# Quantised window attention and a ConvNeXt block on one core: the order of VectorE's five instructions within an attention step

## The chip, the cores and the metric

The kernel runs on one NeuronCore of a Trainium2 chip. A core has five engines, each with a queue of its own that it works through strictly in order: TensorE (PE in the profile, PEld for its weight loads), VectorE (DVE), ScalarE (ACT), GpSimd (POOL) and SyncE (SP, which here only issues transfers). They meet through semaphores alone. The metric is the device time of one execution, in microseconds (us), as the median of several runs; lower is better.

## The reference

The input is 16 images of 192 channels and 56 x 56 pixels. Two layers follow each other: window attention with simulated 8-bit quantisation, then a ConvNeXt block (7x7 depthwise convolution, layer norm, two linear layers, GELU and a response norm). Only the attention is touched, and of it only this core:

```python
attn = jnp.einsum('bhmc,bhnc->bhmn', q, k)     # 12 heads, windows of 7x7 = 49 tokens
bias = fq(bias, axis=0)
attn = fq(attn) + bias[None]                   # fq: round to 8 bits with the maximum of all elements
attn = fq(attn)
attn = jax.nn.softmax(attn, axis=3)
out = jnp.einsum('bhmn,bhnc->bhmc', attn, v)
```

There are 16 x 64 windows. Softmax needs, for each row of 49, the maximum, the exponentials, their sum and a division.

## The kernel before

The program is a row of phases: input, the ranges of q, k and v, their quantisation, the range of the products, **attention**, projection, convolution, MLP. Each phase is a block; its engines' programs are written out by hand, and nothing reorders them.

Attention handles two windows at once (49 of each 64 partitions) for all twelve heads: a tile is 128 partitions by 588 columns. One such pair of windows is an item, 16 items are a unit, and there are 32 units, so 512 items. A loop turn on every engine is two units, 32 steps long and written out in full. In step n each engine does its stages for different items, given by `LAG_A2, LAG_MX, LAG_L, LAG_E, LAG_PV, LAG_N = 1, 2, 3, 4, 6, 7`. In step n:

- TensorE, in this order: the products q k of item n into `p_psum` (line 551 in a helper); the shifted logits of item n-3 into `l_psum` (lines 842 to 846: the logits and the negated maxima are added up by matmuls with the identity), which wait for the maxima of n-3; the 24 matmuls with v for item n-6 into `o_psum` (line 861), which wait for the division of n-7, since there is a single `o_psum`, and for GpSimd's part of n-6; and the transposes of item n-1 into `t_psum` (line 870), which wait for the logits of n-1 and for the maxima of n-2, since there is a single `t_psum`.
- ScalarE: two exponentials of item n-4, to f32 (889) and to f16 (890), and then the rounding of item n to int8, `attn_int` (896).
- GpSimd: `exp_lo`, the difference of the two exponentials of item n-4, in two instructions (819).
- VectorE: the **logits** of item n-1, `logit_int` (915), which read two tiles in SBUF (`attn_int` and the bias) and wait for ScalarE's rounding; the **reciprocals** of the twelve sums of item n-7 (924), which wait for its matmuls with v (semaphore `pv_done`); the **maxima** of item n-2 (930), which read `t_psum` and wait for its transposes (`transposed`); the **division** of item n-7 (939), which reads `o_psum` and writes `a_o` (`norm_done`). After every fourth division a reduction over four items, `o_stat` (945), is taken, and after every sixteenth two tiny instructions more (948 and 950), which let the unit's result be stored.

SyncE loads q, k and v a unit ahead and stores the results; what it waits for are ends of units.

Of the kernel before, what the change touches and what calls it, by code (L numbers as in the profile page):

```python
# [7 lines left out]
ALU = mybir.AluOpType  # L8
# [5 lines left out]
P = 128  # L14
# [6 lines left out]
HEADS, HD = 12, 16  # L21
# [6 lines left out]
UP = UB * PAIRS  # L28
# [32 lines left out]
def chain(eng, sem, start=0):  # L61

    count = [start]

    def link(ins):
        count[0] += 1
        ins.then_inc(sem, 1)
        eng.wait_ge(sem, count[0])
    link.count = count
    return link  # L70
# [46 lines left out]
def col(s, k, rows=P):  # L117
    return s.sc[0:rows, k:k + 1]
# [601 lines left out]
PV0 = 2 * (HD + 1)  # L720

LAG_A2, LAG_MX, LAG_L, LAG_E, LAG_PV, LAG_N = 1, 2, 3, 4, 6, 7
# [7 lines left out]
def phase_attention(s):  # L730

    nc = s.nc
    H1 = HD + 1
    CHUNKS = [(0, 0), (128, 0), (256, 0), (384, 0), (HM - P, 512 - (HM - P))]
    with ExitStack() as c:
# [4 lines left out]
        o = [sb(f"a_o{k}", [P, UP, 2, CK], F32) for k in range(2)]  # L740
# [6 lines left out]
        rec = sb("sum_recip", [P, 12], F32)  # L747
# [5 lines left out]
        po = pb("o_psum", [P, 512], F32)  # L753
        ld = [s.sem(f"a_qk_loaded{k}") for k in range(2)]
        lv = [s.sem(f"a_v_loaded{k}") for k in range(2)]
        st = [s.sem(f"a_stored{k}") for k in range(2)]
# [3 lines left out]
        hid, lod, pvd, nrm = s.sem("hi_done"), s.sem("lo_done"), s.sem("pv_done"), s.sem("norm_done")  # L760
        recd, ostd, ch, ar = s.sem("recip_done"), s.sem("o_stat_done"), s.sem("p4_chain"), s.sem("o_allmax")
# [3 lines left out]
        def steps(eng, step):  # L765

            def turn(i, first):
                for k in range(2):
                    for j in range(UP):
                        step(32 * i + 16 * k + j, 16 * k + j, lambda lag: not first or 16 * k + j >= lag)  # L770
            peeled(eng, IMG, turn)
            for j in range(LAG_N):
                step(TAIL + j, j, lambda lag: lag > j)

        @blk.sync
        def _(sp):
            def store(u, k):
                sp.wait_ge(ostd, u + 1)
                for h in range(2):
                    sp.dma_start(s.od[bass.ds(u, 1)].rearrange("u h n j w f -> (u h) n j w f")[h], o[k][64 * h:64 * h + N]).then_inc(st[k], 16)  # L780

            def unit(i, first):
                for k in range(2):
                    u = bass.ds(2 * i + k, 1)
                    if not first:
                        sp.wait_ge(qk, UP * (2 * i + k - 1))
                    load_qk(s, sp, u, q[k], kt[k], ld[k])
                    if not first:
                        sp.wait_ge(pvd, UP * (2 * i + k - 1))
                    else:  # L790
                        sp.wait_ge(vzero, k + 1)
                    for w in range(2):
                        sp.dma_start(vt[k][64 * w:64 * w + N, w], s.vd[bass.ds(2 * i + k, 1)].rearrange("u o n j f -> (u o) n j f")[w]).then_inc(lv[k], 16)
                    if not first:
                        store(2 * i + k - 2, k)
            peeled(sp, IMG, unit)
            for k in range(2):
                store(UNITS - 2 + k, k)
            for k in range(2):
                sp.wait_ge(st[k], 32 * IMG)  # L800
# [100 lines left out]
        @blk.vector  # L901
        def _(dve):
            v = nc.vector
            v.memset(orun[:], 0.0).then_inc(recd, 1)
            for m in vt + o:
                v.memset(m[:], 0.0).then_inc(vzero, 1)
            dve.wait_ge(vzero, 4)

            def step(n, l, stage):
                if stage(LAG_A2):  # L910
                    m, r = n - LAG_A2, (l - LAG_A2) % 4
                    dve.wait_ge(a1d, m + 1)
                    if stage(LAG_A2 + 4):
                        dve.wait_ge(lgd, m - 3)
                    v.scalar_tensor_tensor(a2[r][:], a1[(l - LAG_A2) % 2][:], col(s, RAT), s.bpart[:], ALU.mult, ALU.add).then_inc(a2d, 1)  # L915
                if stage(LAG_N):
                    m, lm = n - LAG_N, (l - LAG_N) % (2 * UP)
                    k, j = lm // UP, lm % UP
                    dve.wait_ge(pvd, m + 1)
                    if stage(LAG_N + 1):  # L920
                        dve.wait_ge(nrm, m)
                    if j == 0 and stage(LAG_N + 2 * UP):
                        dve.wait_ge(st[k], m - lm)
                    v.reciprocal(rec[:], po[:, 0:12 * H1].rearrange("p (x c) -> p x c", c=H1)[:, :, HD]).then_inc(recd, 1)
                if stage(LAG_MX):
                    m, r = n - LAG_MX, (l - LAG_MX) % 4
                    dve.wait_ge(td, m + 1)
                    if stage(LAG_MX + 4):
                        dve.wait_ge(lgd, m - 3)
                    v.tensor_reduce(nmx[r][:], pt[:, 0:5].rearrange("p c (w n) -> p c w n", w=2)[:, :, :, 0:N], AX.X, ALU.max,  # L930
                                    negate=True).then_inc(mxd, 1)
                if stage(LAG_N):
                    m, lm = n - LAG_N, (l - LAG_N) % (2 * UP)
                    k, j = lm // UP, lm % UP
                    dve.wait_ge(recd, m + 2)
                    src = po[:, 0:6 * PV0].rearrange("p (b w c) -> p b w c", b=6, w=2)[:, :, :, 0:HD]
                    rr = rec[:].rearrange("p (b w) -> p b w", b=6).unsqueeze(3).broadcast_to([P, 6, 2, HD])
                    dst = o[k][:, j].rearrange("p w (b c) -> p b w c", b=6)
                    v.tensor_tensor(dst, src, rr, ALU.mult).then_inc(nrm, 1)  # L939
                if stage(LAG_N):  # L940
                    m, lm = n - LAG_N, (l - LAG_N) % (2 * UP)
                    k, j = lm // UP, lm % UP
                    if j % 4 == 3:
                        dve.wait_ge(nrm, m + 1)
                        v.tensor_reduce(ost[:, j // 4:j // 4 + 1], o[k][:, j - 3:j + 1], AX.XYZ, ALU.max, apply_absolute_value=True).then_inc(ch2, 1)
                    if j == UP - 1:
                        dve.wait_ge(ch2, 5 * unit_of(n, l) + 4)
                        v.tensor_tensor(orun[:], orun[:], ost[:], ALU.max).then_inc(ch2, 1)
                        dve.wait_ge(ch2, 5 * unit_of(n, l) + 5)
                        v.memset(mark[:], 0.0).then_inc(ostd, 1)  # L950

            def unit_of(n, l):

                m, lm = n - LAG_N, (l - LAG_N) % (2 * UP)
                return (m - lm) // UP + lm // UP

            ch2 = s.sem("o_stat_chain")
            mark = sb("mark", [1, 1], F32)
            steps(dve, step)
            dve.wait_ge(ostd, UNITS)  # L960
            link = chain(dve, ch)
            link(v.memset(col(s, T0), 0.0))
            for p0 in (0, 64):
                link(v.tensor_reduce(s.sc[p0:p0 + N, T0:T0 + 1], orun[p0:p0 + N, :], AX.X, ALU.max))
            dve.wait_ge(ar, 1)

            link(v.tensor_tensor(col(s, T1), col(s, T1), col(s, SV), ALU.mult))
            link(v.tensor_scalar(col(s, T1), col(s, T1), AMIN, None, ALU.max))
            link(v.tensor_scalar(col(s, SO), col(s, T1), 1.0 / QMAX, None, ALU.mult))
            link(v.reciprocal(col(s, T2), col(s, T1)))  # L970
            link(v.tensor_tensor(col(s, T2), col(s, T2), col(s, SV), ALU.mult))
            link(v.tensor_scalar(col(s, INVO), col(s, T2), QMAX, None, ALU.mult))
# [876 lines left out]
```

## Time and profile before

| | us |
|---|---|
| median of 3 runs | 5552.63 (5549.53 to 5571.55) |
| profiled execution | 5547.89, span of its trace 5545.9 |
| first and last start of the logits (L915) | 1595.4, 2912.2 |
| VectorE busy in the whole span | 4244.0 (77%) |
| TensorE busy in the whole span | 4071.9 (73%) |
| ScalarE busy | 2965.2 (53%) |
| GpSimd busy | 1516.8 (27%) |

The span is the time from the first to the last instruction of the trace. Attention takes about a quarter of it. The page's chain of what ended last covers other phases, so attention must be read from the order in time of its own instructions: a start, a duration, and in brackets how long the engine was idle before it and who ended that. On VectorE an instruction may start before the recorded end of the one ahead, by some 0.08 us, so steps are measured from start to start.

### The profile page before, as it was taken

To read this page: it belongs to the slowest core of one execution; us is meant where nothing else is said; L and a number is where in the kernel's file an instruction comes from. 1 tells how busy PE (TensorE), PEld (TensorE's weight loads), DVE (VectorE), ACT (ScalarE), POOL (GpSimd) and SP (SyncE) were. 2 spreads that over 40 slices of the span, in tenths; PEclk is the share of its full clock that TensorE was granted. 3 is DMA by queue.
4 is the path that set the end of the run, shared out by engine and by line. 5 is a ranking of instruction groups with operands and counts; after the bars stand their busy time and mean duration, and the time that the engine had idled before them with its cause. 6 is when DMAs were issued, how large, how long until landed. Compare 5 with 4: busy or idle time off the path is not lost. (4 is left out here: it accounts for less than half of the span.)

```text
span 5545.9 us, 116266 instructions
## 1 busy us (share of the span) xinstructions
PE 4071.9 (73%) x40394; PEld 2582.2 (47%) x40394; DVE 4244.0 (77%) x6728; ACT 2965.2 (53%) x5218; POOL 1516.8 (27%) x1842
## 2 busy tenths in 40 slices
PE   0786783444447787777784665999668999999999
PEld 0333453333336666666663443444334454545454
DVE  6898997999989888888895554000189999999985
ACT  0764660000048787787782655444356666666664
POOL 0103330000036555565563221000122222222220
PEclk9998885555579999999996777999879999999999
DMA  7864763333323333333224777788512222222222
GB/s 299 220 180 138 224 220 85 65 66 70 70 54 83 80 79 83 78 80 83 77 67 158 249 273 254 268 289 292 184 63 81 82 84 79 84 80 86 80 75 63
DMA packets 227818, 724.20 MB, mean 131 GB/s; under 512 B 30347, under 2 KB 128139, under 8 KB 206795
## 3 DMA queue, kind: packets, MB, share of 16 engines
q1 hardware_dynamic: 203402, 589.58, 36.5%
q0 software_dynamic: 24128, 130.26, 6.5%
q8 instruction: 245, 4.01, 0.3%
q14 instruction: 43, 0.34, 0.0%
HBM read 428.25 MB, written 291.50 MB: 130 GB/s over the span
## 5 line engine op out<-in xcount | busy, mean ns | idle before, releaser
L819 POOL TENSOR_TENSOR exp_lo<-exp,exp_hi 128x294 f16<-128x294 f32 x1024 | 774.7, 780 | 553.7 <-ACT exp_hi L890 549.8
L896 ACT ACTIVATE attn_int<-p_psum,scalars 128x588 int8<-128x588 f32 x512 | 384.6, 751 | 995.7 <-PE p_psum L551 969.3
L1581 PE MATMUL out_psum<-gelu_hi,w_parts 128*128 128x448 f16 x2016 | 605.7, 355 | 58.1 <-DVE w_parts L1757 30.7
L915 DVE SCALAR_TENSOR_TENSOR logit_int<-attn_int,scalars,bias_products 128x588 f16<-128x588 int8 x512 | 506.3, 989 | 117.7 <-ACT attn_int L896 88.5
L633 PE MATMUL range_psum<-q_diag,k_diag 128*128 128x196 bf16 x1536 | 293.2, 369 | 369.1 <-DVE p_min L679 362.6
L1653 DVE BATCH_NORM_STATS2 ln_stats<-z_img 128x6 f32<-128x192 f32 x448 | 126.0, 344 | 564.2 <-DMA z_img<-zd 563.6
L1617 ACT ACTIVATE gelu_pair<-h_psum,b_rows,w_unscale 128x448 f32<-128x448 f32 x448 | 325.0, 729 | 414.5 <-PE h_psum L1533 249.8
L861 PE MATMUL o_psum<-a_v,exp_hi 128*128 128x34 f16 x6144 | 383.1, 179 | 193.5 <-DVE a_o L939 183.0
L1317 PE MATMUL conv_psum<-c_in,toeplitz 128*128 128x448 f16 (+1 forms) x2304 | 469.3, 366 | 67.4 <-DMA dwb<-in_L_conv_dw_b_dram 67.3
L1533 PE MATMUL h_psum<-ln_parts_T,w_hi 128*128 128x448 f16 x2016 | 494.7, 354 | 18.5 <-DVE w_in L1716 16.5
L1581 PE MATMUL out_psum<-gelu_lo,w_parts 128*128 128x448 f16 x1344 | 476.0, 354 | 0.0
L861 PEld LDWEIGHTS o_psum<-a_v,exp_hi 128*128 128x128 f16 x6144 | 340.5, 96 | 245.8 <-issue 200.2
L633 PEld LDWEIGHTS range_psum<-q_diag,k_diag 128*128 128x128 bf16 x1536 | 223.7, 161 | 438.3 <-DVE p_min L679 428.8
L889 ACT ACTIVATE exp<-l_psum,scalars 128x588 f32<-128x588 f32 x512 | 382.0, 746 | 32.1 <-PE l_psum L846 28.7
L1474 POOL TENSOR_TENSOR ln_parts<-ln_out,ln_parts 128x512 f16<-128x512 f32 x224 | 257.2, 1168 | 504.3 <-DVE ln_parts L1681 504.3
L890 ACT ACTIVATE exp_hi<-l_psum,scalars 128x588 f16<-128x588 f32 x512 | 393.0, 767 | 0.0
L1331 ACT ACTIVATE c_out<-conv_psum,dwb,conv_unscale 128x448 f32<-128x448 f32 x192 | 223.6, 1165 | 312.7 <-PE conv_psum L1317 312.7
L861 PE MATMUL o_psum<-a_v,exp_lo 128*128 128x34 f16 x6144 | 381.2, 179 | 1.5 <-issue 1.5
L1317 PEld LDWEIGHTS conv_psum<-c_in,toeplitz 128*128 128x128 f16 x2304 | 223.6, 98 | 312.9 <-DMA dwb<-in_L_conv_dw_b_dram 41.1
L1533 PE MATMUL h_psum<-ln_parts_T,w_lo 128*128 128x448 f16 x1344 | 365.8, 354 | 0.0
L930 DVE TENSOR_REDUCE neg_max<-t_psum 128x10 f16<-128x490 f16 x512 | 327.1, 639 | 28.7 <-PE t_psum L870 16.3
L861 PEld LDWEIGHTS o_psum<-a_v,exp_lo 128*128 128x128 f16 x6144 | 337.8, 96 | 7.8 <-issue 7.0
(313 smaller groups left out, 9684.7 us busy)
## 6 DMA issues: line engine op xcount, KB each, us to landing
k_diag<-kd SPq DMA_DIRECT2D x128, 384.0 KB, 5.3
toeplitz<-gd SPq DMA_DIRECT2D x48, 1024.0 KB, 16.8
yd<-y_out POOLq DMA_DIRECT2D x16, 2880.0 KB, 28.0
c_in<-yd SPq DMA_DIRECT2D x24, 1920.0 KB, 9.5
zd<-c_out POOLq DMA_DIRECT2D x24, 1792.0 KB, 13.9
z_img<-zd SPq DMA_DIRECT2D x16, 2688.0 KB, 9.4
x_chunk<-in_x_dram SPq DMA_DIRECT2D x12, 3136.0 KB, 9.9
x_img<-in_x_dram SPq DMA_DIRECT2D x16, 2352.0 KB, 16.0
```

The source lines that it names most:

```text
L633: last = nc.tensor.matmul(ps[:, x % 2, y // 2, y % 2 * 256:y % 2 * 256 + HG * N], kt[k][:, g].rearrange("p o n -> p (o n)")[:, j::UP], q[k ...
L819: last = nc.gpsimd.tensor_tensor(el[r][:, :, 2 * a, 0:N], src[:, :, a], eh[r][:, :, 2 * a, 0:N], ALU.subtract)
L861: last = nc.tensor.matmul(po[:, b * PV0:(b + 1) * PV0], x[r][:, b, a:a + 2].rearrange("p a n -> p (a n)"), rhs, start=a == 0 and x is eh, ...
L889: nc.scalar.activation(e[r % 2][:], pl[:, bank, 0:HM], ACT.Exp, scale=col(s, S2))
L890: nc.scalar.activation(eh[r][:, :, 0:3:2].rearrange("p b a n -> p a b n")[:, :, :, 0:N], pl[:, bank, 0:HM].rearrange("p (a b n) -> p a b n ...
L896: nc.scalar.activation(a1[l % 2][:].rearrange("p (g n) -> p g n", g=G), pp[:, 0:G, 0:HG * N], ACT.Copy, scale=col(s, CP)).then_inc(a1d, 1)
L915: v.scalar_tensor_tensor(a2[r][:], a1[(l - LAG_A2) % 2][:], col(s, RAT), s.bpart[:], ALU.mult, ALU.add).then_inc(a2d, 1)
L930: v.tensor_reduce(nmx[r][:], pt[:, 0:5].rearrange("p c (w n) -> p c w n", w=2)[:, :, :, 0:N], AX.X, ALU.max, negate=True).then_inc(mxd, 1)
L1317: last = nc.tensor.matmul(out[:, :, lo:hi], tp[k][:, w, ch, 2 - d, :], yi[k][:, :, ch, yy, lo + d:hi + d], start=x == 0 and part == 0, sto ...
L1533: last = nc.tensor.matmul(ph[:, y % 3, 0:TCH], w, xx, start=x == 0, stop=x == 4)
L1581: last = nc.tensor.matmul(po[:, t, 0:TCH], w, hx[:, f, cols], start=f == 0 and x == 0, stop=f == NF - 1 and x == len(steps) - 1)
L1617: nc.scalar.activation(h[y // 2 % 3][:, y % 2], ph[:, y % 3, 0:TCH], ACT.Gelu, scale=k1[:], bias=b1[:, f:f + 1]).then_inc(hd, 1)
```

## The change

VectorE's instructions within a step are written in another order. Before: logits, reciprocals, maxima, division. After: reciprocals, logits, division, maxima. Every instruction keeps its operands and its waits; no buffer, no lag and no other engine's program changes. `o_stat` stays last in its step.

```diff
             def step(n, l, stage):
+                if stage(LAG_N):
+                    m, lm = n - LAG_N, (l - LAG_N) % (2 * UP)
+                    k, j = lm // UP, lm % UP
+                    dve.wait_ge(pvd, m + 1)
+                    if stage(LAG_N + 1):
+                        dve.wait_ge(nrm, m)
+                    if j == 0 and stage(LAG_N + 2 * UP):
+                        dve.wait_ge(st[k], m - lm)
+                    v.reciprocal(rec[:], po[:, 0:12 * H1].rearrange("p (x c) -> p x c", c=H1)[:, :, HD]).then_inc(recd, 1)
                 if stage(LAG_A2):
...
-                    dve.wait_ge(pvd, m + 1)
-                    if stage(LAG_N + 1):
-                        dve.wait_ge(nrm, m)
-                    if j == 0 and stage(LAG_N + 2 * UP):
-                        dve.wait_ge(st[k], m - lm)
-                    v.reciprocal(rec[:], po[:, 0:12 * H1].rearrange("p (x c) -> p x c", c=H1)[:, :, HD]).then_inc(recd, 1)
+                    dve.wait_ge(recd, m + 2)
+                    src = po[:, 0:6 * PV0].rearrange("p (b w c) -> p b w c", b=6, w=2)[:, :, :, 0:HD]
...
+                    v.tensor_tensor(dst, src, rr, ALU.mult).then_inc(nrm, 1)
                 if stage(LAG_MX):
...
-                if stage(LAG_N):
...
-                    v.tensor_tensor(dst, src, rr, ALU.mult).then_inc(nrm, 1)
```

VectorE's queue before, in a step that ends with the reduction over four items and at the start of the next. Here L915 is the logits, L924 the reciprocals, L930 the maxima, L939 the division, L945 the reduction:

```order
L915 SCALAR_TENSOR_TENSOR logit_int<-attn_int,scalars,bias_products 128x588 [waits logits_done,a1_done]
L924 RECIPROCAL sum_recip<-o_psum 128x12 [waits norm_done,pv_done]
L930 TENSOR_REDUCE neg_max<-t_psum 128x10 [waits logits_done,transposed]
L939 TENSOR_TENSOR a_o<-o_psum,sum_recip 128x6x2x16 [waits recip_done]
L945 TENSOR_REDUCE o_stat<-a_o 128x1 [waits norm_done]
L915 SCALAR_TENSOR_TENSOR logit_int<-attn_int,scalars,bias_products 128x588 [waits logits_done,a1_done]
```

The same place after the change, where the lines are L918 for the reciprocals, L924 for the logits, L932 for the division and L938 for the maxima:

```order
L918 RECIPROCAL sum_recip<-o_psum 128x12 [waits norm_done,pv_done]
L924 SCALAR_TENSOR_TENSOR logit_int<-attn_int,scalars,bias_products 128x588 [waits logits_done,a1_done]
L932 TENSOR_TENSOR a_o<-o_psum,sum_recip 128x6x2x16 [waits recip_done]
L938 TENSOR_REDUCE neg_max<-t_psum 128x10 [waits logits_done,transposed]
L945 TENSOR_REDUCE o_stat<-a_o 128x1 [waits norm_done]
L918 RECIPROCAL sum_recip<-o_psum 128x12 [waits norm_done,pv_done]
```

The logits now stand between the reciprocals and the division, the maxima behind the division, and a step begins with the wait for the matmuls with v (`pv_done`) instead of the wait for the rounding (`a1_done`).

## Rows read from the trace of the kernel before

**Rows 1.** First line of the page.

```profile
span 5545.9 us, 116266 instructions
```

**Rows 2.** Busy time of the engines over the attention stretch, with its columns.

```profile
core 0: us, PE busy (x) PEld busy (x) DVE busy (x) ACT busy (x) POOL busy (x), PEclk, DMA share, GB/s
1595.00:2926.00 1331.00, 1043.45 (x22524) 844.48 (x22522) 1153.37 (x2243) 1053.65 (x1535) 774.66 (x1024) 0.95 0.31 78
```

**Rows 3.** Waits in the attention stretch: us in total, times, longest us.

```profile
PE o_psum L861 <- DVE a_o L939: 183.0, 437, 1.8
```

**Rows 4.** The reductions over four items, all of them: durations, first and last start.

```profile
L945 DVE TENSOR_REDUCE o_stat<-a_o x128: 952/953/955, 1615.0 to 2924.5; 128x1 f32<-128x768 f32 x128
```

**Rows 5.** Instructions of VectorE in time, one group of four steps: start us, us.

```profile
2112.34 0.34 DVE L939 TENSOR_TENSOR a_o<-o_psum,sum_recip 128x192 f32<-128x192 f32 x1
2112.70 0.95 DVE L945 TENSOR_REDUCE o_stat<-a_o 128x1 f32<-128x768 f32 x1
2113.57 0.82 DVE L915 SCALAR_TENSOR_TENSOR logit_int<-attn_int,scalars,bias_products 128x588 f16<-128x588 int8 x1
2114.31 0.23 DVE L924 RECIPROCAL sum_recip<-o_psum 128x12 f32<-128x12 f32 x1
2114.45 0.61 DVE L930 TENSOR_REDUCE neg_max<-t_psum 128x10 f16<-128x490 f16 x1
2114.98 0.34 DVE L939 TENSOR_TENSOR a_o<-o_psum,sum_recip 128x192 f32<-128x192 f32 x1
2115.24 1.05 DVE L915 SCALAR_TENSOR_TENSOR logit_int<-attn_int,scalars,bias_products 128x588 f16<-128x588 int8 x1
...
2116.55 0.67 DVE L930 TENSOR_REDUCE neg_max<-t_psum 128x10 f16<-128x490 f16 x1
2117.14 0.35 DVE L939 TENSOR_TENSOR a_o<-o_psum,sum_recip 128x192 f32<-128x192 f32 x1
...
2118.42 0.23 DVE L924 RECIPROCAL sum_recip<-o_psum 128x12 f32<-128x12 f32 x1
...
2121.57 0.33 DVE L939 TENSOR_TENSOR a_o<-o_psum,sum_recip 128x192 f32<-128x192 f32 x1
```

**Rows 6.** The same steps: TensorE's matmuls with v and transposes; then GpSimd's rows.

```profile
2117.63 0.18 PE L861 MATMUL o_psum<-a_v,exp_hi 128*128 128x34 f16 x1 [0.22 <-DVE a_o L939]
...
2118.23 0.44 PE L870 MATMUL t_psum<-ident_f,logit_int 128*128 128x128 f16 x5
...
2114.04 1.62 POOL L819 TENSOR_TENSOR exp_lo<-exp,exp_hi 128x294 f16<-128x294 f32 x2 [0.75 <-ACT exp_hi L890]
...
2121.11 1.41 POOL L819 TENSOR_TENSOR exp_lo<-exp,exp_hi 128x294 f16<-128x294 f32 x2 [0.75 <-ACT exp_hi L890]
```

**Rows 7.** Three meetings of the logits with GpSimd, from VectorE's and GpSimd's instructions in time.

```profile
2103.81 1.94 POOL L819 TENSOR_TENSOR exp_lo<-exp,exp_hi 128x294 f16<-128x294 f32 x2 [0.75 <-ACT exp_hi L890]
2103.82 1.35 DVE L915 SCALAR_TENSOR_TENSOR logit_int<-attn_int,scalars,bias_products 128x588 f16<-128x588 int8 x1
...
2106.02 0.81 DVE L915 SCALAR_TENSOR_TENSOR logit_int<-attn_int,scalars,bias_products 128x588 f16<-128x588 int8 x1
2106.05 2.06 POOL L819 TENSOR_TENSOR exp_lo<-exp,exp_hi 128x294 f16<-128x294 f32 x2 [0.30 <-ACT exp_hi L890]
...
1601.83 1.94 POOL L819 TENSOR_TENSOR exp_lo<-exp,exp_hi 128x294 f16<-128x294 f32 x2 [9.04 <-ACT exp_hi L890]
1602.33 0.86 DVE L915 SCALAR_TENSOR_TENSOR logit_int<-attn_int,scalars,bias_products 128x588 f16<-128x588 int8 x1 [0.76 <-ACT attn_int L896]
```

**Rows 8.** VectorE at the end of a unit.

```profile
2102.47 0.95 DVE L945 TENSOR_REDUCE o_stat<-a_o 128x1 f32<-128x768 f32 x1
```

**Rows 9.** VectorE after the stop at a loop turn.

```profile
2088.29 0.83 DVE L915 SCALAR_TENSOR_TENSOR logit_int<-attn_int,scalars,bias_products 128x588 f16<-128x588 int8 x1 [5.29 <-ACT attn_int L896]
2089.26 0.23 DVE L924 RECIPROCAL sum_recip<-o_psum 128x12 f32<-128x12 f32 x1
...
2090.38 0.35 DVE L939 TENSOR_TENSOR a_o<-o_psum,sum_recip 128x192 f32<-128x192 f32 x1
```

More of the change, by code:

```diff
@@ L918, in step @@
                     k, j = lm // UP, lm % UP
-                    dve.wait_ge(pvd, m + 1)
-                    if stage(LAG_N + 1):
-                        dve.wait_ge(nrm, m)
-                    if j == 0 and stage(LAG_N + 2 * UP):
-                        dve.wait_ge(st[k], m - lm)
-                    v.reciprocal(rec[:], po[:, 0:12 * H1].rearrange("p (x c) -> p x c", c=H1)[:, :, HD]).then_inc(recd, 1)
+                    dve.wait_ge(recd, m + 2)
+                    src = po[:, 0:6 * PV0].rearrange("p (b w c) -> p b w c", b=6, w=2)[:, :, :, 0:HD]
+                    rr = rec[:].rearrange("p (b w) -> p b w", b=6).unsqueeze(3).broadcast_to([P, 6, 2, HD])
+                    dst = o[k][:, j].rearrange("p w (b c) -> p b w c", b=6)
+                    v.tensor_tensor(dst, src, rr, ALU.mult).then_inc(nrm, 1)
                 if stage(LAG_MX):
@@ L931, in step @@
                                     negate=True).then_inc(mxd, 1)
-                if stage(LAG_N):
[L933 to L938, printed above, removed]
-                    v.tensor_tensor(dst, src, rr, ALU.mult).then_inc(nrm, 1)
                 if stage(LAG_N):
```

## The prediction

> **What bounds the kernel now.** The first view is the busy time by stretch: in the 1331 us of attention VectorE is busy for 1153, ScalarE for 1054, TensorE for 1043 [rows 2]. No engine is full, so a loop of waits between them sets the pace. The second view is the waits: TensorE stands 183.0 us, in 437 of 512 steps, before its matmuls with v until VectorE's division is done [rows 3]. The change brings that division forward, past the maxima. What it pays is read from the third view, the instructions in time.
>
> All numbers of a step are distances from start to start. I call the start of a division N. From N, the matmuls with v start 0.49 later (2117.14 to 2117.63) [rows 5, 6]; the transposes start 1.09 after N (2118.23), are 0.44 long, and the next maxima start 0.04 after that, at N + 1.57 (2114.98 to 2116.55) [rows 5, 6]; the next division is 0.59 after them (2116.55 to 2117.14) [rows 5]. So **before** there is a loop division, matmuls with v, transposes, maxima, division, of 1.57 + 0.59 = 2.16 us, and 2114.98 to 2117.14 is just that. Of the other loop, the reciprocals may start at N + 1.28 (2117.14 to 2118.42), the end of the matmuls with v [rows 5].
>
> A group of four steps, from the division ahead of one reduction to that ahead of the next, is 2112.34 to 2121.57 = 9.23 [rows 5]: the step with the reduction takes 2.64 (2112.34 to 2114.98), two take 2.16, one takes 2.27, in which the logits stood behind GpSimd. 68 of the 96 groups that do not hold a unit's end take 9.22 to 9.30; the mean over all is (2924.5 - 1615.0) / 127 = 10.31 [rows 4], since 15 loop turns hold a stop of some 5 us [rows 9] and 31 groups a unit's end.
>
> **The change part by part.** Nothing is added or removed; 512 steps are reordered.
>
> *The loop that goes.* The maxima no longer stand ahead of the division. They run at N + 0.26 (as 2114.98 to 2115.24 for what followed a division without waiting) and are over at about N + 0.87, before the transposes that need their buffer (N + 1.09) and before the shifted logits, which come after those. They are hidden under the 1.28 us of the matmuls with v. The loop of 2.16 is gone.
>
> *The loop that takes its place.* The logits now stand between the reciprocals and the division: reciprocals, 0.15 (0.14 in 2114.31 to 2114.45, and 0.01 for a start out of a wait), logits, 0.74 (2113.57 to 2114.31), division, 1.28 or 1.29, reciprocals. Sum 0.15 + 0.74 + 1.29 = **2.18 us** [rows 5], against 2.16. A plain step thus gains nothing: the 0.59 of the maxima left the loop and the 0.74 of the logits entered it, while the 0.29 between the ends of the two TensorE stages was won.
>
> *The step with the reduction.* After N: 0.26, maxima 0.52 (2114.45 to 2114.98 pipelined), reduction 0.87 (2112.70 to 2113.57), reciprocals 0.14, logits at N + 1.79, division at N + 2.53 if nothing stops them [rows 5]. That is 0.11 less than the 2.64 of before. Four steps: 2.53 + 3 x 2.18 = 9.07, which is 0.16 under 9.23.
>
> *What stops the logits.* The logits and GpSimd's two instructions don't run at the same time. Logits that start 0.01 after GpSimd take 1.35 instead of 0.82, and GpSimd 1.94 instead of 1.41; logits that start 0.03 before GpSimd take 0.81 and GpSimd 2.06; logits that start 0.50 after it, near the end of its first instruction, slip between the two: 0.86 [rows 7]. So a tie costs 0.53, while to be 0.03 ahead or 0.50 behind costs nearly nothing. The Trainium skill, SBUF — State Buffer, in its section on the ports, says the same in kind: a VectorE instruction with two inputs in SBUF and a GpSimd instruction exclude each other for a whole instruction, and who starts first has the port. By a bandwidth that is merely shared the sum would be the 9.07 above in every group; by the page's lock it hangs on who is first, and the trace agrees with the lock (1.35 against 0.82). What follows uses the rows only.
>
> GpSimd starts 3.97 after the division two of its steps back (2117.14 to 2121.11) [rows 5, 6], since that division releases, through TensorE, the rounding and then the exponentials; the change leaves this chain as it is. In plain steps the logits start at N + 1.43 + 2.18 = N + 3.61, thus 0.36 before GpSimd: free. After a reduction, GpSimd comes 3.97 - 2.18 = 1.79 after N, and the logits at N + 1.79: **a tie**, to within what I can read. By the first row pair of [rows 7] I give it to GpSimd: + 0.54. Then division at N + 3.07; the following logits at 3.07 + 1.44 = 4.51, which is 0.54 after GpSimd's 3.97, so between its two instructions; the third and fourth steps are free. Group: 3.07 + 3 x 2.18 = **9.61**, + 0.38 on 9.23.
>
> *The ends of units.* From the reduction to the next logits it is 2102.47 to 2103.82 = 1.35, and to the next reduction (2112.70) 10.23, with a tie in it [rows 5, 7, 8]; 9 groups read so, 13 are 0.5 shorter, without the tie, and 9 longer. After: 0.26 + 0.52 + 1.35 + 0.14 = N + 2.27 for the logits, 0.48 behind GpSimd: it slips in for 0.04. Division at 3.05, group 3.05 + 6.54 = 9.59. Gain 0.64 in 9, 0.13 in 13, and I take 0.3 in the other 9: 5.8 + 1.7 + 2.7 = 10 us.
>
> *The loop turns.* TensorE stops for about 5 us; before, the first reciprocals (2089.26) wait for the matmuls with v, the maxima for the transposes, and the division starts at 2090.38, 1.12 later [rows 9]. After it is 0.15 + 0.74 = 0.89: 0.23 less, and the next step starts without the wait for transposes. I take 0.4 for each of 15: 6 us. The logits wait longer there for the reciprocals, but are ready in time.
>
> **Sum.** 68 groups x 0.38 = + 26; ends of units - 10; loop turns - 6; 13 disturbed groups at half the tie + 2: **+ 12 us**. The trace's span of 5545.9 [rows 1] lies 2.0 under its own execution's time of 5547.89, which gives 5560; the median of the runs is 4.7 above that execution: about **5564 us**.
>
> **The rivals.**
> *Who wins the tie: VectorE.* Then the group is 9.07 and 68 x 0.16 = 11 us are gained, with 10 and 6 as above and 1 for the others: - 28, 5525 us. For it: the two starts are equal by my rows, and 0.03 ahead is enough. Against: 0.01 or 0.02 more anywhere in the loop pulls GpSimd forward relative to the logits. Since by this case the next step is a tie again, it needs all ties.
> *Starts that cost more.* The maxima take 0.67 out of a wait and 0.61 without (0.59 and 0.53 to the division) [rows 5]: 0.06 for a start out of a wait. If the reciprocals, which now wait in each step, hand this to the logits, 512 x 0.06 = + 31: 5595 us.
> *The gap is missed: slower.* After a lost tie the next logits arrive 0.54 after GpSimd's start; I have seen 0.50 slip in. If the second GpSimd instruction (0.7 long) is already in, they wait till shortly before its end (in the tie 0.53 were waited for a first instruction of 1.41 / 2 = 0.7, so 0.2 before it): 1.41 - 0.2 - 0.54 = 0.67, and the step behind meets GpSimd's first instruction for 0.2 more. The group is then some 10.5, + 1.25 x 68 = 85, less 14: + 71, 5624 us. It decides at the point where the logits arrive later than about 0.6 after GpSimd.
> *The wait for the division was worth its 183 us.* If TensorE's wait were the bound, moving the division by 0.59 would give 0.3 or more in each step, 150 us. Against it: TensorE waits for a division that itself waits for the matmuls one step earlier; I give it 2 in 100.
>
> **How the numbers follow.** Forecast with the tie lost 0.50; tie won 0.22; dearer starts 0.14; gap missed 0.12; the large gain 0.02. A measurement of this kernel can tell about 0.5%, or 28 us, from no change: 5525 and 5580 are the bounds. The forecast lies within them; the tie won lies on the lower bound, half of it is counted as faster (0.11), and with the large gain and surprises of that sign I say 0.17. Slower: dearer starts, gap missed and a little of the forecast's upper end, 0.30. The rest, 0.53, is within. The range takes in the tie won with some margin and the dearer starts, 5515 to 5602, and leaves out the missed gap and the large gain.
>
> **What the profile after would show.** Plain steps of 2.17 to 2.20 between divisions; maxima starting 0.26 after the division; reciprocals always waiting for the matmuls with v; TensorE's wait for the division smaller in no great measure, since the loop is as long; the logits behind the reduction of about 1.35 (tie lost) or 0.82 (tie won); those one step later 0.82 to 0.86 (gap) or 1.4 (missed). The forecast is wrong if plain steps are not near 2.18, or if GpSimd no longer starts 3.97 after a division.

## The result and the profile after

The changed kernel takes 5644.02 us (median of 4 runs, 5626.26 to 5646.43), the kernel before 5558.41 in the same comparison: ratio 1.0145, 95% interval 1.0114 to 1.0176. It is slower, by about 86 us between the medians, and lies above the predicted range, which ended at 5602. The profiled execution has a span of 5641.8, 95.9 more than that of before [rows 1].

First, where the time lies. The busy times of the attention stretch and the 128 reductions over four items (columns as in [rows 2] and [rows 4]) of the changed kernel:

```profile
1595.00:3030.00 1435.00, 1052.87 (x22522) 852.53 (x22522) 1142.57 (x2251) 1053.10 (x1535) 908.70 (x1027) 0.93 0.29 73
```

```profile
L945 DVE TENSOR_REDUCE o_stat<-a_o x128: 934/942/953, 1614.0 to 3015.8; 128x1 f32<-128x768 f32 x128
```

From the first to the last reduction it is now 1401.8 us, before 1309.5: 92 of the 96 us are in this loop. VectorE, ScalarE and TensorE are as busy as before to within 1% (1143, 1053, 1053 us); only GpSimd has gone from 775 to 909. Its rows on the two pages, first before, then after (busy us, mean ns | idle before):

```profile
L819 POOL TENSOR_TENSOR exp_lo<-exp,exp_hi 128x294 f16<-128x294 f32 x1024 | 774.7, 780 | 553.7 <-ACT exp_hi L890 549.8
```

```profile
L819 POOL TENSOR_TENSOR exp_lo<-exp,exp_hi 128x294 f16<-128x294 f32 x1024 | 905.6, 907 | 514.4 <-ACT exp_hi L890 510.7
L924 DVE SCALAR_TENSOR_TENSOR logit_int<-attn_int,scalars,bias_products 128x588 f16<-128x588 int8 x512 | 501.2, 979 | 2.2 <-ACT attn_int L896 2.2
```

The logits have not become longer: 979 ns on average, 989 before. Without GpSimd's subtractions they take 816 and 827 ns (experiments 2 and 1), so what they wait for GpSimd inside their own duration is the same in both orders, some 0.16 us each or 83 us over 512. It has moved to a place where it counts.

The waits in the attention stretch (us in total, times, longest) show the new loop: the reciprocals now stand before the matmuls with v, and TensorE still stands before the division, longer than before [rows 3]:

```profile
DVE sum_recip L918 <- PE o_psum L861: 272.4, 402, 6.6
PE o_psum L861 <- DVE a_o L932: 250.5, 426, 1.8
```

**Two patterns.** Of the 96 groups of four steps without a unit's end, 24 take 9.6 to 9.85 us and 27 take 10.4 to 10.6 (before, 66 took 9.2 to 9.35). Here is one of the first kind, VectorE in time (start us, us), with the first two instructions of GpSimd that it meets behind it. Compare [rows 5]:

```profile
1783.24 0.35 DVE L932 TENSOR_TENSOR a_o<-o_psum,sum_recip 128x192 f32<-128x192 f32 x1
1783.51 0.66 DVE L938 TENSOR_REDUCE neg_max<-t_psum 128x10 f16<-128x490 f16 x1
1784.08 0.94 DVE L945 TENSOR_REDUCE o_stat<-a_o 128x1 f32<-128x768 f32 x1
1784.94 0.22 DVE L918 RECIPROCAL sum_recip<-o_psum 128x12 f32<-128x12 f32 x1
1785.08 1.29 DVE L924 SCALAR_TENSOR_TENSOR logit_int<-attn_int,scalars,bias_products 128x588 f16<-128x588 int8 x1
1786.29 0.34 DVE L932 TENSOR_TENSOR a_o<-o_psum,sum_recip 128x192 f32<-128x192 f32 x1
...
1787.58 0.23 DVE L918 RECIPROCAL sum_recip<-o_psum 128x12 f32<-128x12 f32 x1 [0.37 <-PE o_psum L861]
1787.75 0.83 DVE L924 SCALAR_TENSOR_TENSOR logit_int<-attn_int,scalars,bias_products 128x588 f16<-128x588 int8 x1
1788.50 0.35 DVE L932 TENSOR_TENSOR a_o<-o_psum,sum_recip 128x192 f32<-128x192 f32 x1
...
1792.91 0.35 DVE L932 TENSOR_TENSOR a_o<-o_psum,sum_recip 128x192 f32<-128x192 f32 x1
```

```profile
1785.01 1.94 POOL L819 TENSOR_TENSOR exp_lo<-exp,exp_hi 128x294 f16<-128x294 f32 x2 [0.42 <-ACT exp_hi L890]
1787.21 1.96 POOL L819 TENSOR_TENSOR exp_lo<-exp,exp_hi 128x294 f16<-128x294 f32 x2 [0.26 <-ACT exp_hi L890]
```

The logits behind the reduction (1785.08) lose the tie against GpSimd (1785.01) and take 1.29; the next (1787.75) start 0.54 after GpSimd and slip between its two instructions, 0.83. The distances between divisions are 3.05, 2.21, 2.20, 2.21, in all 9.67. This is the predicted pattern (9.61), to 0.06.

And here is one of the second kind, which the prediction does not have:

```profile
2229.64 0.34 DVE L932 TENSOR_TENSOR a_o<-o_psum,sum_recip 128x192 f32<-128x192 f32 x1
...
2231.09 1.35 DVE L924 SCALAR_TENSOR_TENSOR logit_int<-attn_int,scalars,bias_products 128x588 f16<-128x588 int8 x1
2232.37 0.34 DVE L932 TENSOR_TENSOR a_o<-o_psum,sum_recip 128x192 f32<-128x192 f32 x1
...
2233.83 1.14 DVE L924 SCALAR_TENSOR_TENSOR logit_int<-attn_int,scalars,bias_products 128x588 f16<-128x588 int8 x1
2234.89 0.34 DVE L932 TENSOR_TENSOR a_o<-o_psum,sum_recip 128x192 f32<-128x192 f32 x1
...
2236.34 1.36 DVE L924 SCALAR_TENSOR_TENSOR logit_int<-attn_int,scalars,bias_products 128x588 f16<-128x588 int8 x1
2237.63 0.34 DVE L932 TENSOR_TENSOR a_o<-o_psum,sum_recip 128x192 f32<-128x192 f32 x1
```

```profile
2231.09 1.94 POOL L819 TENSOR_TENSOR exp_lo<-exp,exp_hi 128x294 f16<-128x294 f32 x2 [0.79 <-ACT exp_hi L890]
2233.61 1.94 POOL L819 TENSOR_TENSOR exp_lo<-exp,exp_hi 128x294 f16<-128x294 f32 x2 [0.58 <-ACT exp_hi L890]
2236.34 1.94 POOL L819 TENSOR_TENSOR exp_lo<-exp,exp_hi 128x294 f16<-128x294 f32 x2 [0.80 <-ACT exp_hi L890]
```

Steps alternate: 2.73, 2.52, 2.74, and 2.51 to the next. (That next step holds a reduction, and keeps the rhythm: behind a step of 2.74 GpSimd starts early, and the logits come 0.62 after it, at 2239.47 against 2238.85, and slip in between its two instructions.) GpSimd still starts 3.97 after a division (2229.64 to 2233.61, 2232.37 to 2236.34). So a step of length P puts the logits after it at N + P + 1.46 against GpSimd at N + 3.97. If P is 2.52 that is a tie, 0.53 is waited, and the step becomes 2.21 + 0.53 = 2.74. After a step of 2.74 the logits come 0.22 after GpSimd and wait the remaining 0.3: 2.52, and the next is a tie again. Two steps in a row sum to 2.21 + (3.97 - 1.46) + 0.53 = 5.25. In 134 places of the trace two steps in a row, each over 2.4, sum to 5.23 to 5.29; in 3 places before. (Both must be over 2.4, since 3.05 + 2.21 of the first kind gives 5.26 too.) **The waiting keeps itself alive**: each wait lengthens the step by just what makes the next logits meet GpSimd again. Plain steps of 2.21 don't meet it (0.3 ahead), but nothing inside the pattern leads back to them except the chance that a tie falls the other way.

**Where the second kind starts: at the loop turns.** TensorE's stop there makes a step of 7 to 8.5 us. The second step behind it holds a reduction. Here is one turn, VectorE and then GpSimd:

```profile
2201.69 0.23 DVE L918 RECIPROCAL sum_recip<-o_psum 128x12 f32<-128x12 f32 x1 [5.79 <-PE o_psum L861]
...
2207.26 0.76 DVE L924 SCALAR_TENSOR_TENSOR logit_int<-attn_int,scalars,bias_products 128x588 f16<-128x588 int8 x1
...
2209.40 1.37 DVE L924 SCALAR_TENSOR_TENSOR logit_int<-attn_int,scalars,bias_products 128x588 f16<-128x588 int8 x1
```

```profile
2207.28 4.06 POOL L819 TENSOR_TENSOR exp_lo<-exp,exp_hi 128x294 f16<-128x294 f32 x4 [0.50 <-ACT exp_hi L890]
```

The logits behind the reduction start together with GpSimd and win (0.76, and the step is 2.52); the next ones lose (1.37). So it goes almost every time: the step with the reduction is 2.52 behind all 14 such stops, in 12 of them with a start within 0.03 of GpSimd's, and in 13 the alternation follows. Five of the 13 end in the same group, when a tie falls to VectorE. The other eight last until an irregular stop of TensorE, the next turn or the end.

**The end of a unit** is the third finding. Before, behind the reduction of [rows 8]:

```profile
2103.46 0.16 DVE L948 TENSOR_TENSOR o_run<-o_run,o_stat 128x4 f32<-128x4 f32 x1
```

After (VectorE, then GpSimd):

```profile
2169.51 0.94 DVE L945 TENSOR_REDUCE o_stat<-a_o 128x1 f32<-128x768 f32 x1
2170.49 0.70 DVE L948 TENSOR_TENSOR o_run<-o_run,o_stat 128x4 f32<-128x4 f32 x1
2171.25 0.06 DVE L950 MEMSET mark<- 1x1 f32 x1
```

```profile
2170.44 1.41 POOL L819 TENSOR_TENSOR exp_lo<-exp,exp_hi 128x294 f16<-128x294 f32 x2 [0.42 <-ACT exp_hi L890]
```

The running maximum over units (948), four columns wide, also reads two tiles in SBUF. With the maxima ahead of it, it starts with GpSimd and takes 0.69 to 0.71 instead of 0.16, in 20 of the 32 units. The median step at a unit's end is 3.72 us, against 3.05 predicted.

A second loss hangs on it. Here are such a step and the two behind it (columns as in [rows 2]; the third number from the end is the granted clock):

```profile
1772.14:1775.86 3.72, 2.17 (x54) 1.68 (x48) 3.60 (x8) 3.57 (x6) 2.76 (x4) 1.00 0.44 142
1775.86:1778.08 2.22, 1.73 (x33) 1.74 (x34) 1.83 (x5) 0.18 (x1) 1.41 (x2) 0.73 0.46 179
1778.08:1781.03 2.95, 2.95 (x49) 2.10 (x49) 1.84 (x5) 2.37 (x4) 0.23 (x1) 0.63 0.45 183
```

TensorE is busy for only 2.17 of the 3.72 us, then the granted clock falls for a while from 1.00 to 0.50 (from the level of 2.4 GHz to that of 1.2), TensorE is busy throughout, and a step takes 2.95 instead of 2.21. This happens behind 12 of the 31 ends, all with the long step, and costs some 8 us; before, it happens behind 5.

### The profile page after: what moved, and what is told of

Read it like the earlier page. It is cut to its first block and busy times, and to the rows that moved or that the text cites. A ratio compares the mean times of both kernels' runs of the same rounds, so it can differ in the third digit from the quotient of the medians.

```text
span 5641.8 us, 116266 instructions
## 1 busy us (share of the span) xinstructions
PE 4085.3 (72%) x40394; PEld 2593.7 (46%) x40394; DVE 4230.7 (75%) x6728; ACT 2965.3 (53%) x5218; POOL 1649.2 (29%) x1842
## 5 line engine op out<-in xcount | busy, mean ns | idle before, releaser
L819 POOL TENSOR_TENSOR exp_lo<-exp,exp_hi 128x294 f16<-128x294 f32 x1024 | 905.6, 907 | 514.4 <-ACT exp_hi L890 510.7
L924 DVE SCALAR_TENSOR_TENSOR logit_int<-attn_int,scalars,bias_products 128x588 f16<-128x588 int8 x512 | 501.2, 979 | 2.2 <-ACT attn_int L896 2.2
L679 DVE TENSOR_TENSOR p_max<-range_psum,p_max 128x1568 f32<-128x1568 f32 x192 | 341.2, 1777 | 0.0
```

What stands on the lines that cost most here:

```text
L679: v.tensor_tensor(e[:, g], ps[:, x % 2].rearrange("p a (b c) -> p (a b) c", b=2)[:, :, 0:HG * N], e[:, g], op).then_inc(done, 1)
L819: last = nc.gpsimd.tensor_tensor(el[r][:, :, 2 * a, 0:N], src[:, :, a], eh[r][:, :, 2 * a, 0:N], ALU.subtract)
```

## The experiments

Each kernel was timed beside the kernel before; ratios are to that, with their 95% intervals. Theory A: logits and GpSimd's subtractions exclude each other and fall into step. Rival B: the new loop is slow by itself.

**1 and 2: no subtractions.** In both orders, GpSimd's two instructions become one on a single element; the kernels leave out the low part of the exponentials.

```diff
-                    for a in range(2):
-                        last = nc.gpsimd.tensor_tensor(el[r][:, :, 2 * a, 0:N], src[:, :, a], eh[r][:, :, 2 * a, 0:N], ALU.subtract)
+                    last = nc.gpsimd.tensor_tensor(tick[:, r:r + 1], tock[:], tock[:], ALU.subtract)
```

> The kernel before, with GpSimd's two subtractions per step replaced by one on a single element; the low part of the exponentials stays zero, so that part of the computation is left out. Theory A (the changed kernel is slow because logits and GpSimd's subtractions exclude each other and fall into step): before loses its few waits too, a group of four steps is 2.64 + 3 x 2.16 = 9.12 instead of 9.24, time some 10 to 25 us under the kernel before. Rival B (the new loop through the logits is slow by itself, GpSimd plays no part): within 5 us of before.

> The changed order, with the same part left out: GpSimd's subtractions are one on a single element. Theory A: the difference between the orders vanishes: plain steps 2.21, the step with the reduction 2.51, group 9.14, time within 15 us of the run before without subtractions. Rival B: the changed order stays 60 us or more slower than it.

Before without subtractions: 5526.07 us, 0.997 (0.9948 to 0.9992). Changed without subtractions: 5536.35 us, 0.9988 (0.997 to 1.0006). The 1.45% have become 0.2%, with intervals that overlap; from first to last reduction it is 1297.0 us in the changed order,

```profile
L945 DVE TENSOR_REDUCE o_stat<-a_o x128: 939/943/953, 1615.6 to 2912.6; 128x1 f32<-128x768 f32 x128
```

and 1295.7 in the order of before. The group of four reads as theory A has it, 2.52 + 2.21 + 2.20 + 2.21 = 9.14:

```profile
1777.11 0.35 DVE L932 TENSOR_TENSOR a_o<-o_psum,sum_recip 128x192 f32<-128x192 f32 x1
...
1779.63 0.35 DVE L932 TENSOR_TENSOR a_o<-o_psum,sum_recip 128x192 f32<-128x192 f32 x1
...
1781.84 0.35 DVE L932 TENSOR_TENSOR a_o<-o_psum,sum_recip 128x192 f32<-128x192 f32 x1
...
1784.04 0.35 DVE L932 TENSOR_TENSOR a_o<-o_psum,sum_recip 128x192 f32<-128x192 f32 x1
...
1786.25 0.35 DVE L932 TENSOR_TENSOR a_o<-o_psum,sum_recip 128x192 f32<-128x192 f32 x1
```

Rival B has fallen. These two don't tell which instruction of VectorE is stopped, only that GpSimd's work is needed for the loss. It could also reach the loop another way, since TensorE's weight loads for the matmuls with v wait for `exp_lo`. That wait was 38.6 us in all before and is 55.1 in the changed kernel, so this way explains at most 17 of the 92 us. Nearly all of it lies at units' ends, and it is gone in experiment 9.

**3 and 4: the same subtractions in one, and in four instructions**, in the changed order.

```diff
+                    last = nc.gpsimd.tensor_tensor(el[r][:, :, 0:3:2, 0:N], src, eh[r][:, :, 0:3:2, 0:N], ALU.subtract)
...
+                    for a in range(2):
+                        for b in (0, 3):
+                            last = nc.gpsimd.tensor_tensor(el[r][:, b:b + 3, 2 * a, 0:N], src[:, b:b + 3, a], eh[r][:, b:b + 3, 2 * a, 0:N], ALU.subtract)
```

> The changed order, GpSimd's two subtractions in one instruction of twice the size. Theory A: two steps in a row sum to 2.21 + (3.97 - 1.45) + h, h being what a tie costs; h grows from 0.53 to about 1.2, so steps alternate around 2.95 instead of 2.63 wherever they are in step, and the tie behind a reduction costs 1.2: 60 to 120 us slower than the changed kernel, 5700 to 5760. Rival B: no change, 5640.

> The changed order, GpSimd's subtractions in four instructions of half the size. Theory A: h is about 0.2; a step of 2.52 is followed by one of 2.4, which is too short to meet GpSimd again, so steps fall back to 2.21 and a group is 9.2 to 9.5: 5550 to 5590. Rival B: no change, 5640, or slower by GpSimd's added instructions.

One instruction: 5696.21 us, 1.0256 (1.0203 to 1.0308), just under the expected 5700. The tie now costs 1.0 (logits of 1.82 that start 0.07 after GpSimd, so 1.06 for a full tie; VectorE, then GpSimd):

```profile
1751.03 1.82 DVE L923 SCALAR_TENSOR_TENSOR logit_int<-attn_int,scalars,bias_products 128x588 f16<-128x588 int8 x1
```

```profile
1750.96 1.27 POOL L818 TENSOR_TENSOR exp_lo<-exp,exp_hi 128x588 f16<-128x588 f32 x1 [0.55 <-ACT exp_hi L889]
```

24 groups read 11.6, steps of 3.06 and 2.73 in turn: a pair of 5.79, where 4.72 + 1.06 = 5.78. Four instructions: 5568.9 us, 1.0045 (1.0026 to 1.0064), within the expectation. The most common group is 2.77 + 3 x 2.21 = 9.4, and no two steps over 2.4 sum to 5.23 to 5.29. The same work in other pieces moves the time over 127 us, in the way the wait for one piece of it says.

**5 and 9: the end of a unit.** First the element's write behind the running maximum was suspected, then the running maximum itself.

```diff
-                        v.memset(mark[:], 0.0).then_inc(ostd, 1)
+                        v.tensor_reduce(mark[:], ost[0:1, :], AX.X, ALU.max).then_inc(ostd, 1)
...
-                        v.tensor_tensor(orun[:], orun[:], ost[:], ALU.max).then_inc(ch2, 1)
+                        v.tensor_reduce(both[1 - k][:, 1], both[k][:].rearrange("p a b -> p b a"), AX.X, ALU.max).then_inc(ch2, 1)
```

> The changed order; at a unit's end the one-element memset (line 950) is replaced by a one-line reduction from o_stat to the same element. Theory A2: the memset is stopped by GpSimd's instruction for 0.53 (from o_run to it 0.75 instead of 0.22 in 20 of 32 units), which pushes the logits 0.5 back and into GpSimd's second instruction; a reduction with one input isn't stopped: the step at a unit's end shrinks from 3.72 to about 3.1 to 3.2, 10 to 25 us in all. Rival: the delay is the wait for the semaphore after o_run and stays: no change.

> The changed order; at a unit's end the running maximum (line 948), an instruction with two inputs in SBUF, is taken by a reduction over one tile that holds both. Theory A3: it was this instruction, 0.70 long instead of 0.16, that GpSimd stopped, since behind the maxima it starts with GpSimd; it goes back to 0.16 to 0.2, the step at a unit's end from 3.72 to about 3.05 (17 us in all), and the step behind it slips between GpSimd's two instructions more often, so that fewer units run at 10.5 a group: 5590 to 5630 in all. Rival: the delay moves to whatever stands there (the element's write behind it), no change, 5640.

Experiment 5: 5638.47 us, 1.0165 (1.013 to 1.0201), no change, and the step at a unit's end stays at 3.71: theory A2 was wrong. I had read the gap from one start to the next and had not looked at the duration of the instruction between them, which was 0.70. Experiment 9: 5611.74 us, 1.0121 (1.0104 to 1.0138). VectorE at a unit's end there:

```profile
1859.48 0.94 DVE L944 TENSOR_REDUCE o_both<-a_o 128x1 f32<-128x768 f32 x1
1860.45 0.16 DVE L947 TENSOR_REDUCE o_both<-o_both 128x4 f32<-128x8 f32 x1
1860.66 0.06 DVE L949 MEMSET mark<- 1x1 f32 x1
```

With one input it is 0.16 again, the median step 3.06, and the 31 groups at units' ends take 317.8 us in all, 340.6 in the changed kernel. That is 23 of the 26 us by which the loop, from first to last reduction, is shorter (1376.1 against 1401.8). The granted clock no longer falls behind any of the 31 ends. The two traces differ by 41.7 in all; the other 16 lie outside this loop. The hope that fewer groups would alternate was not met: 26 still take 10.4 to 10.6. Its trace says why: the alternation begins behind all 14 stops at the loop turns, and only once elsewhere. In the changed kernel 13 of its 16 beginnings lie behind such a stop. So the ends of units are a loss of their own, and seldom the way into the pattern.

**10: both remedies in the changed order.**

> The changed order with both: four shorter subtractions and the running maximum by one input. If the two are all that the order lost against the kernel before, it comes to within 10 us of it, about 17 under the same with four subtractions alone: 5540 to 5560. If something else is left, 5565 or more.

5555.45 us, 1.0014 (1.0003 to 1.0025), within 10.5 us of the 5544.95 of before in that comparison. With both remedies all but about a tenth of the loss is gone (0.14% of 1.45%). They were not tried in the order of before, so what they would give there is open.

**6, 7 and 8: other orders of the same five instructions**, with no other change. Experiment 6 is the division ahead of the maxima alone, 8 the reciprocals ahead of the logits alone.

> One part of the change alone: division ahead of the maxima, the logits stay first (logits, reciprocals, division, maxima). Theory A: the loop division, matmuls with v, reciprocals, division is 1.28 + 0.14 to 0.3 = 1.4 to 1.6 and doesn't hold the logits, so TensorE's own order (2.0 to 2.1 a step) or VectorE's sum is next: plain steps 2.05, group 8.7 to 9.1, and a wait for GpSimd is taken from slack: 5490 to 5545. Rival B (any order with the division ahead of the maxima is slow): 5600 or more.

> Reciprocals, division, logits, maxima: the logits leave the loop through the division but not the place ahead of the maxima. Theory A: loop 1.28 + 0.3 = 1.6; the maxima end at division + 1.65, so the transposes wait for them (they could start at + 1.09): plain steps 2.1 to 2.3, 5500 to 5570. Rival B: as slow as the changed kernel, 5640.

> The other part of the change alone: only the reciprocals move ahead of the logits (reciprocals, logits, maxima, division). Loop reciprocals, logits, maxima, division, matmuls: 0.17 + 0.75 + 0.52 + 1.28 = 2.72 or more in every step: 10.9 a group and up, 5760 to 5850, by theory A with the logits and GpSimd falling into step when the gap to it allows. Rival B, in which the place of the maxima is what costs: faster than the changed kernel.

Experiment 6: 5525.15 us, 0.9957 (0.9939 to 0.9976). Experiment 7: 5529.44, 0.9968 (0.9946 to 0.9989). Experiment 8: 5845.82, 1.0536 (1.0499 to 1.0574), steps of 2.79 and 3.04. So bringing the division forward was worth something, 0.4%; bringing the reciprocals ahead of the logits, and so the logits into the loop, was the harm, with the division forward or not. Plain steps in experiment 6 are 1.85 to 1.93 us, faster than the 2.05 I had thought TensorE's order would allow, but 102 of its logits still take over 1.25.

**11 and 12: those orders with the two remedies.**

> Logits, reciprocals, division, maxima, with four shorter subtractions and the running maximum by one input: the ties that still cost 0.5 in one or two of four steps cost 0.2. Plain steps 1.9, group 8.4 to 8.8, ends of units about 9.3: 5470 to 5515. If ties are not what holds this order, no better than the order alone, 5525.

> Reciprocals, division, logits, maxima with the same two. This order has few ties (17 logits over 1.25 us), its steps are held by the transposes that wait for the maxima: group 9.0 to 9.1, ends 9.6: 5505 to 5530. If four instructions cost GpSimd more than they bring, 5530 or more.

Experiment 11: **5491.28 us, 0.9907 (0.988 to 0.9934)**, faster than both kernels, and some 30 us under experiment 6, which has the same order without the remedies. One group of it, 8.87 from division to division:

```profile
1770.84 0.36 DVE L932 TENSOR_TENSOR a_o<-o_psum,sum_recip 128x192 f32<-128x192 f32 x1
...
1772.55 1.11 DVE L915 SCALAR_TENSOR_TENSOR logit_int<-attn_int,scalars,bias_products 128x588 f16<-128x588 int8 x1
1773.58 0.22 DVE L924 RECIPROCAL sum_recip<-o_psum 128x12 f32<-128x12 f32 x1
1773.84 0.36 DVE L932 TENSOR_TENSOR a_o<-o_psum,sum_recip 128x192 f32<-128x192 f32 x1
...
1775.69 0.36 DVE L932 TENSOR_TENSOR a_o<-o_psum,sum_recip 128x192 f32<-128x192 f32 x1
...
1779.71 0.36 DVE L932 TENSOR_TENSOR a_o<-o_psum,sum_recip 128x192 f32<-128x192 f32 x1
```

A plain step is 1.85 and a tie costs 0.3. Experiment 12: 5539.78 us, 0.9984 (0.9968 to 1.0), missed: I expected 5505 to 5530. Its maxima stand behind the logits, TensorE's transposes wait 130.9 us for them in 246 steps (118.2 in experiment 7), and most of its groups lose a tie of 0.3 that experiment 7 did not have.

## Why the prediction was wrong

*The loops.* Right. The loop through the maxima went, that through the logits came. A plain step is 2.21, not 2.18: the logits start 0.17 after waiting reciprocals, not 0.15, and take 0.75. Over the 96 groups without a unit's end that is 3 x 0.03 x 96 = 9 us. Experiment 2 gives the whole group without GpSimd at 9.14, against 9.07. Two counts were off and weigh little: the trace of before has 66 groups of 9.22 to 9.30, not 68, and 14 turns with a stop, not 15.

*The tie behind the reduction.* Right in that it is a tie and in its price: 3.05 against 3.07, then the gap, then two free steps. Who wins was right only in part. Of the 96 steps with a reduction away from units' ends, 35 take 3.0 to 3.1, the tie lost; in 17 it was won, and 21 more take 2.5 to 2.6 too, 18 of them through the gap. The row pair that gave it to GpSimd could not decide this: among all logits that start within 0.03 of GpSimd in the changed kernel, 65 lose and 19 win.

*The four steps as the only pattern.* **This step failed.** I began the group with a step of 2.18, found that it ends with one, and took that for the kernel's course. I did not ask what a step of another length leads to. A step of 2.52, which is what a reduction gives when the tie behind it is won, leads to a tie, to 2.74, to 2.52. The 27 groups in this pattern cost 1.28 each over 9.23, 35 us, the 24 of the first kind 11, and the rest lies in groups that mix the two or hold a loop turn: the 96 groups take 1061.6 us against 984.8, 77 more, where my terms give 22 (26 for the tie, 6 less for the loop turns, 2 for disturbed groups).

*The rivals.* The tie won was priced at - 28 us because I had it win every time. The rival even says that the next step is a tie again, and did not ask what follows when that one is lost. It is the way into the slow pattern: what I took for the favourable case is part of the loss. The missed gap was priced at 5624, nearest to the result, at a chance of 0.12. It does occur, nine times behind units' ends (logits 0.67 to 0.69 after GpSimd's start, where I had put the edge at about 0.6), but what repeats itself is not the chain that I had worked out there; that its group of 10.5 is also the length of the alternating one is chance. The dearer starts were worth 0.03, not 0.06. The large gain did not come: the division is brought forward, yet waits for reciprocals that wait for the matmuls one step earlier, as said.

*The ends of units.* Wrong in sign: - 10 us foreseen, + 16 measured (340.6 against 324.7). I listed the two tiny instructions in the 1.35 between starts, taken from a place where GpSimd did not touch them, and did not see that one of them has two inputs in SBUF and was being moved to where GpSimd starts. By experiment 9 that is 23 us, some 13 of it the longer steps themselves (0.67 in 20 of them) and some 8 the lower clock behind them, which had no term in my sum; without it the ends would have gained 7, and without GpSimd's subtractions they do gain 7 (303.6 us in experiment 2 against 310.5 in experiment 1).

*The loop turns.* A gain of 6 was foreseen; none is seen. The 14 groups that hold a stop take 8.7 us more in all than before, and without GpSimd's subtractions the groups at this place of the loop still don't gain: 237.4 us for 16 in experiment 2, 235.1 in experiment 1. The groups with a stop vary from 15.0 to 16.2 us in those two traces, so the few us are not resolved. What the turns do is start the slow pattern, as shown above.

*The port.* That a VectorE instruction with two inputs in SBUF and a GpSimd instruction that reads SBUF shut each other out, as the Trainium skill says (SBUF — State Buffer, SBUF: two separate sides), is borne out in its detail: the instruction of four columns with two inputs takes 0.70, the same maximum with one input 0.16. The rule was right and was applied to one of the two instructions that it covers.

## What to carry to other kernels

Where two engines exclude each other and one of them times the other, don't follow one course of the schedule: write the next step's length as a function of this one's, and look for every length that reproduces itself. A tie that the rows can't decide belongs in the forecast with both outcomes mixed, since each may happen in turn. Keep an instruction that may be stopped off the loop that sets the pace; the same waits of 83 us in all cost some 13 (0.3%, experiment 1) in the order of before, where the logits stood first in the step with slack behind them. When an instruction is moved, list all that now starts at another moment, the tiny ones too, with how many inputs in SBUF each has; and cut the other engine's instruction into pieces, since what is waited for is one piece.

## What the runs showed of the hardware

- The wait is for one GpSimd instruction, not for its work: a tie costs 0.53 with two instructions of 0.7, 1.06 with one of 1.27, 0.2 to 0.3 with four. Where the line runs is sharp: in the changed kernel's trace logits that start 0.53 to 0.65 after the first of two instructions lose nothing, and the ten that start 0.66 to 0.69 after it take 1.34 to 1.38, having waited for the second.
- Which of two that start together goes first can't be told from recorded starts within 0.03 us of each other: in the changed kernel's trace GpSimd went first 65 times, VectorE 19.
- A VectorE instruction on 128 x 4 elements with two inputs in SBUF takes 0.70 instead of 0.16 when GpSimd is at work; the stop is inside its recorded duration, and no idle time or wait shows it.
- Behind the 20 steps of 3.71 to 3.74 us at units' ends (TensorE busy for 2.17 in the one shown) the granted clock fell from 1.00 to 0.50 in 12 cases, and the second step behind took 2.65 to 2.95 instead of 2.21. Behind the 31 ends of 3.05 to 3.23 in experiment 9 it never fell.
- TensorE can work through its four stages for a step in 1.85 us at a granted clock of 1.00, the level of 2.4 GHz. That is seen in experiments 6 and 11, where it is VectorE that has no idle time left (busy for 8.73 of the 8.87 us of the group shown). The 2.16 of the kernel before was a loop, not TensorE's speed.
